# The pitch in DRAM between the rows of delta*u that one load of a selective scan reads

## The reference, cut to what matters

```python
delta = softplus(einsum('kblr,krc->kblc', dpart, dt_w) + 2 * dt_b)
# for each token, in the order of direction k:
dA    = exp(d[..., None] * A_neg)                 # A_neg = -exp(A_logs)
state = dA * state + (d * uu)[..., None] * b      # b: the token's 16 values of B
y     = einsum('kbcn,kbn->kbc', state, c)         # c: the token's 16 values of C
```

## Time and profile before

| | us |
|---|---|
| runs | 19140.31, 19143.47, 19148.17 |
| median | 19143.47 |
| profiled execution | 19173.11 |
| its span, from the first to the last instruction | 19171.4 |

### The profile page before, as it was taken

How to read it: one execution, slowest core, us unless ns; L and a number is a source line. 1 busy time by engine, 2 the same in 40 slices (tenths; PEclk the granted TensorE clock), 3 DMA queues, 4 the chain that set the end, 5 groups by cost and what they waited for, 6 DMA issues and landing times. The chain is left out here.

```text
span 19171.4 us, 359393 instructions
## 1 busy us (share of the span) xinstructions
PE 14991.3 (78%) x130080; PEld 11045.3 (58%) x130080; DVE 11710.9 (61%) x10632; ACT 7349.9 (38%) x12681; POOL 6928.4 (36%) x3199
## 2 busy tenths in 40 slices
PE   7899898989997534444888888888888888854489
PEld 5666666666665211122777677767777677732267
DVE  5666666666665666565667676667677667732232
ACT  4444444444443333333444444444444444411100
POOL 1000000000000233335777677767777677721100
PEclk9999999999998766676777777777777777765699
DMA  5222222222223555657999999899889999954411
GB/s 123 58 59 59 63 54 59 59 63 59 59 53 89 130 139 139 149 133 171 209 208 210 211 209 208 207 210 209 207 209 211 208 210 210 210 129 115 115 48 40
DMA packets 1692801, 2640.22 MB, mean 138 GB/s; under 512 B 1081676, under 2 KB 1245260, under 8 KB 1667404
## 3 DMA queue, kind: packets, MB, share of 16 engines
q1 hardware_dynamic: 1680332, 2551.26, 56.3%
q0 software_dynamic: 12288, 86.71, 2.1%
HBM read 2110.03 MB, written 556.32 MB: 139 GB/s over the span
## 5 line engine op out<-in xcount | busy, mean ns | idle before, releaser
L1680 DVE TENSOR_TENSOR_SCAN L2.h<-L2.ps,L2.db 128x912 f32<-128x912 f32 x2688 | 5514.0, 2056 | 2416.1 <-POOL L2.db L1545 2320.6
L1545 POOL TENSOR_TENSOR L2.db<-L2.du,L2.bt 128x896 f32<-128x896 f32 x2688 | 5576.7, 2093 | 2388.2 <-DMA L2.du<-du 2306.2
L1568 PE MATMUL L2.ps<-L2.dm,L2.wa 32*128 32x112 f32 (+2 forms) x24192 | 4522.0, 346 | 1132.1 <-DVE L2.h L1680 1005.5
L1568 PEld LDWEIGHTS L2.ps<-L2.dm,L2.wa 32*128 32x128 f32 x24192 | 4169.2, 258 | 1838.8 <-DVE L2.h L1680 1294.7
L1620 ACT ACTIVATE L2.ps<-L2.ps 128x896 f32<-128x896 f32 x2688 | 2426.0, 903 | 4607.2 <-PE L2.ps L1568 4606.8
L1580 PE MATMUL L2.ps<-L2.h,L2.cd 128*8 128x96 f32 x50176 | 2575.8, 362 | 4.2 <-DVE L2.h L1680 4.2
L1580 PEld LDWEIGHTS L2.ps<-L2.h,L2.cd 128*8 128x8 f32 x50176 | 1443.6, 108 | 583.8 <-DVE L2.h L1680 4.3
L1137 POOL TENSOR_TENSOR L2p.work<-L2p.work,L2p.xc 128x784 f32<-128x784 f32 x192 | 451.3, 2350 | 1659.2 <-DVE L2p.work L1300 1659.2
L314 POOL TENSOR_TENSOR L1.x_res<-L1.x_res,L1.ob 96x3136 f32 (+1 forms) x16 | 95.4, 5976 | 2584.8 <-ACT L1.qv L457 2584.8
L366 PE MATMUL L1.p_proj<-L1.xt,L1.w_hi 128*96 128x448 f32 x3024 | 826.9, 383 | 194.3 <-DVE L1.xt L560 167.4
L366 PE MATMUL L0.p_proj<-L0.xt,L0.w_hi 128*96 128x448 f32 x3024 | 824.2, 382 | 193.9 <-DVE L0.xt L560 167.4
(11 more groups left out here) (242 smaller groups left out, 20801.6 us busy)
## 6 DMA issues: line engine op xcount, KB each, us to landing
L2.du<-du SPq DMA_DIRECT2D x2688, 448.0 KB, 11.1
L2.dm<-d SPq DMA_DIRECT2D x896, 336.0 KB, 10.8
du<-L2p.work SPq DMA_DIRECT2D x128, 784.0 KB, 7.6
y<-L2.ysum SPq DMA_DIRECT2D x896, 84.0 KB
L0.left<-table SPq DMA_DIRECT2D x48, 1176.0 KB
L0.right<-table SPq DMA_DIRECT2D x48, 1176.0 KB
L1.left<-table SPq DMA_DIRECT2D x48, 1176.0 KB
L1.right<-table SPq DMA_DIRECT2D x48, 1176.0 KB
```

The source lines that it names most:

```text
L1545: pool.tensor_tensor(db[:, n % RB, :, 2:ROW], du[:, n % RD, :].rearrange("p (c t) -> p c t", t=SPAN), row, ALU.mult)\
L1568: mm = pe.matmul(decays[n % RA][:, a:b], wa[rows, j, :], dm[rows, j, a - lo:b - lo], start=True, stop=True)
L1680: dve.tensor_tensor_scan(h[:, half, u * UNIT:(u + 1) * UNIT, :].rearrange("p c t -> p (c t)"), decays[n % RA], db[:, n % RB, :, :].rearran ...
```

## The change

The tensor `du` is allocated with 896 floats (`UNIT * SPAN`, 3584 bytes) more behind each row of (direction, image, copy). The store and the load skip them. So the 16 rows of a load lie 2412032 bytes apart instead of 2408448. The same values are stored and read in the same order by the same instructions; the padding is never written or read. Tensors allocated after `du` move by 64 x 3584 bytes.

```diff
--- before.py
+++ after.py
@@ -1075,7 +1075,8 @@
                     sp.wait_ge(du_done, q)
                     for at, b, c, size in runs(pr, i):
                         for copy in range(COPIES):
-                            sp.dma_start(du_dram[k, b, copy, spans, c:c + size, :].rearrange("s c t -> c s t"),
+                            rows = du_dram[k, b, copy, 0:NSPANS * CH * SPAN].rearrange("(s c t) -> c s t", c=CH, t=SPAN)
+                            sp.dma_start(rows[c:c + size, spans, :],
                                          one[n % 2][at:at + size, span].rearrange("p (s t) -> p s t", t=SPAN))\
                                 .then_inc(du_stored[n % 2][half], 16)
                     sp.wait_ge(lo_done, q)
@@ -1451,7 +1452,7 @@
 
             def load_du(k, s, half, u):
                 c = half * HALF + u * UNIT
-                rows = du_dram[k].rearrange("b o s c t -> (b o) s (c t)")
+                rows = du_dram[k, :, :, 0:NSPANS * CH * SPAN].rearrange("b o (s n) -> (b o) s n", s=NSPANS)
                 rows = rows[:, s, c * SPAN:(c + UNIT) * SPAN] if isinstance(s, int) else \
                     rows[:, bass.ds(s, 1), c * SPAN:(c + UNIT) * SPAN].rearrange("r a n -> r (a n)")
                 src = bass.AP(tensor=rows.tensor, offset=rows.offset,
@@ -2050,7 +2051,7 @@
     z, xc = (nc.dram_tensor(n, (PAIRS, 128, 3, TOK), F32).ap() for n in ("z", "xc"))
     wa = nc.dram_tensor("wa", (DIRS, 128, SET * 128), F32).ap()
     d = nc.dram_tensor("d", (DIRS, NSPANS, SETS, 2, BATCH, SET, SPAN), F32).ap()
-    du = nc.dram_tensor("du", (DIRS, BATCH, COPIES, NSPANS, CH, SPAN), F32).ap()
+    du = nc.dram_tensor("du", (DIRS, BATCH, COPIES, NSPANS * CH * SPAN + UNIT * SPAN), F32).ap()
     bc = nc.dram_tensor("bc", (2, DIRS, BATCH, STATES, TOK), F32).ap()
     y = nc.dram_tensor("y", (DIRS, BATCH, TOK, CH), F32).ap()
     taps = [[nc.dram_tensor(f"taps{n}_{k}", (D1, LAGS), F32).ap() for k in range(2)] for n in range(2)]
```

## The result

| | before | after |
|---|---|---|
| median of the runs, us | 19142.56 (19132.33 to 19170.48, 8 runs) | 19199.33 (19181.35 to 19218.27, 8 runs) |
| profiled execution, us | 19173.11 | 19181.35 |

The ratio is 1.0029 [1.0018, 1.004]: the change makes the kernel 0.29% slower. The forecast was 17790.

What follows compares the result with a forecast made beforehand. DMA's handling of `du` was taken to bound the scan pass; with cheaper packets a half-span falls from 35.26 to 29.2 us (28.7 PE cycle, 0.5 SyncE), times 224 saves 1357 us: 17816, at the median's level 17790; range 17560 to 19200.

Steps and rivals of the forecast that it cites:

- What bounds the kernel: Scan pass: its end is set by how fast the DMA engines get through `du`, a full queue; half-span 35.26 us.
- (a): Stage before the pass: delta*u stores go to other addresses, hidden, taken as 0; 0.26 ms either way if not hidden.
- (b): `du` loads in the scan pass: the new pitch spreads the rows' addresses, a packet falls from 232 to 140 ns.
- 16 rows agree modulo 16384: `du` loads: at the old pitch all engines ask the same fraction of memory's parts, the supposed cause of 232 ns.
- burst of 140 ns: First `du` packets after the queue ran empty, 12104.6 to 12105.2: 140 ns each, taken as the unhindered price.
- Rival 2: `du` loads: nothing gained; limit on the writing side or in dealing 16 repeated rows to 128 partitions; chance 0.27.
- The Trainium skill's rule on pitches: Counter-evidence for `du` loads: only pitches of 2 MiB and up fell; by it the gain is 0, not 1.36 ms.
- Rival 3: `du` loads: spread rows serve engines unevenly, 6 ns more on the mean packet gives 19285 us; chance 0.13.
- The cycle through PE: Scan pass with cheap `du`: PE bounds next, six sum intervals 18.2 plus 10.5, so 28.7 us a half-span.
- four scans: Half-span after the sums: scans of units 9, 10, 11 and 0, 4 x 2.06 = 8.2 us of the 10.5.
- SyncE's order: Scan pass: y's stores and `cd` loads delay unit 4's `du` load; mostly hides, 0.5 us added, 29.2 in all.
- the 12.8 us to unit 4's landing: SyncE's queue after the last sum: 8.1 + 4.7 us remain; GpSimd at most about 2 us late, PE three units ahead.

Runs made afterwards that it cites:

- e1: Kernel before, each `du` load reading 128 different rows, one per partition, instead of 16 rows eight times each (other values reach the scan): 18591.58 us.
- q2: Kernel before with the eight `cd` loads moved in SyncE's list from behind unit 3's `du` load to behind unit 11's: 18605.79 us, ratio 0.9733.
- p2: Kernel before, stores and allocation kept, only the `du` loads reading at the new pitch (displaced values): 19206.01 us, ratio 1.003.
- e2: Kernel before, all 128 partitions of a `du` load reading one and the same 3584 bytes (other values reach the scan): 18757.47 us.
- e3: Kernel before, each `du` load reading 32 different rows, four times each, 688128 bytes apart (other values reach the scan): 18660.80 us.
- e4: Kernel before, each `du` load reading 16 rows eight times each, but rows lying 3584 bytes apart (other values reach the scan): 19043.16 us.
- s2: Kernel before with four copies of delta*u in DRAM, y's stores and `cd` loads spread behind units 5, 7, 9, 11: 18619.90 us, ratio 0.9728.
- r1: Kernel before with four copies of delta*u in DRAM instead of two, so loads read 32 rows four times each: 19361.35 us, ratio 1.0113.
- p1: Kernel before at the old pitch, with the padding all behind `du` so only later tensors move: 19144.59 us, ratio 0.9998.
- p0: The changed kernel run once more, against the kernel before: 19197.67 us, ratio 1.0022.
- r2: Kernel before with four copies of delta*u in DRAM and the change's 3584 bytes behind each row: 19522.39 us, ratio 1.0194.
- s1: Kernel before, y's stores and `cd` loads spread, one store and two loads behind units 5, 7, 9, 11: 18707.65 us, ratio 0.9769.

## Why the prediction was wrong, point by point

**What bounds the kernel: right in part.** `du`'s packets through the DMA engines hold the pass: cheaper ones gave 590 us of it in e1. But the queue wasn't full throughout: SyncE's order alone gave 565 us in q2, with `du` packets at the old price.

**(a), the stores at nothing: right.** GpSimd's first product starts at 8957.8 instead of 8962.1, and with the loads' pitch alone (p2) the whole slowdown is there.

**(b), 232 to 140 ns: wrong, and the step that sank the forecast.** At the new pitch a `du` packet costs what it did, 227 ns alone and 236.3 instead of 236.9 over the pass. I read "16 rows agree modulo 16384" as the cause since it held wherever 232 ns was seen. The number of outer rows and repeats held there too, and I had no row that parted the two. e2, e3 and e4 part them, all against me. The burst of 140 ns in the earlier trace rows was rightly what a `du` packet can take alone (141 ns in e2 and e3), but it says nothing on why it doesn't; and as the price of the whole pass it was too low, since e1's packets average 176 there. Rival 2 had the place: not the addresses, but how 16 repeated rows are dealt out to 128 partitions. Its evidence, `dm` at half rate, was in the prediction and deserved more than 0.27. It isn't as clean as I wrote, though: `dm`'s loads also read each of 32 rows twice (line 1442), so its 64 partitions alone aren't shown to be the cause. Whether it also gives the full rate with 32 rows depends on which engine fills which partitions, and that no run shows. The Trainium skill's rule on pitches, which spoke against me (DMA: Bandwidth & Descriptors, "Latency and other measured facts"), was right that this pitch has no large cost to mend, by e3 and e4; it holds nothing on the 0.3% of this pad or the 0.8% with four copies.

**Rival 3, slower: its sign was right, its place not.** It had `du` packets 6 ns dearer by uneven service, 19285 us. `du` stayed within 1 ns; `dm` rose by 9. I priced the pad only for the load that it belongs to, and not for the loads that run beside it. That 19199.33 lies within the stated range, 0.67 us under its upper end of 19200, is luck: the forecast was a gain, and nothing in its sum gives a loss of 57 us.

**The cycle through PE, 28.7 us: near, with its second half too short.** s2 came to 29.8 us a half-span in the mean and 29.25 in the median, with GpSimd's wait for `du` down to 179 us, though its `du` packets took 190 ns and not 140. Averaged over s2's trace, the six intervals with sums take 17.7 us, where I had 18.2, and the rest of the half-span 12.1, where I had 10.5. I let four scans set the pace of that rest. In the half-span shown it is mostly PE's own work, 10.53 of 12.03 us, with 27 decays at the low clock in 6.05 us and one wait for the scan of 1.5.

**SyncE's order, 0.5 us: mis-sized.** With cheap packets and the old order a half-span is 33.2 us (r1) and 32.6 (e1); spreading y and `cd` takes 3.4 us off r1 (s2). At the old packet price it is worth 2.5 (q2). I let the 12.8 us to unit 4's landing hide behind units in hand and looked at unit 4 alone; units 3, 4 and 5 all come late, by 2.4, 1.9 and 2.0 us on average in e1. The trace of before had it too, 1.0, 3.0 and 2.2 us at these units, had I averaged over all half-spans and not read one. Had (b) held, the change would have come near what e1 gave, 18592, and not 17790.

**Open:** what in 16 rows of 8 repeats costs the 90 ns, on the side that writes or in the dealing out; why 3584 bytes are worse than 0, 4096 or 32768, and whether `dm` alone pays for it; and which engine serves which partitions in the 16-row pattern.

## What to carry to other kernels

When a load reads a few rows many times over into 128 partitions, suspect the shape of its pattern before its addresses, and try it with another number of outer rows: 16 rows of 8 ran at 232 ns a packet, 32 of 4 at 141. A property that holds wherever the slowness is seen is no cause until a row or a run has it without the slowness. In a queue that is full on average, look for what is issued just before it runs dry: moving eight small loads out of the way gave 2.7%, nine times what the change's pitch cost.

## What the runs showed of the hardware, unexpected

- Loads whose 128 partitions all read the same 3584 bytes run at full rate while they are alone: 141 ns a packet, 419 GB/s (e2). Over the whole pass they are a little dearer than with 128 different rows: 190 ns against 176 (e1).
- 16 rows read 8 times each take 233 ns a packet alone (e4), 32 rows read 4 times each 141 (e3), with the same bytes, packet size and destination.
- With a pad of 3584 bytes in one tensor's pitch, packets read from another tensor were slower by 9 ns of 407 (before and p1 against after and p0); with 32 rows a load it made both kinds some 8 ns slower and cost 0.8% of the kernel (r1, r2).
- Large packets were dearer with small transfers spread among them: `du` packets took 237 ns with y's four stores and the eight `cd` loads each in one block (q2) and 253 with both spread (s1).
- Doubling 154 MB of stores in pieces of 448 bytes took 647 us of a stage whose DMA share had been 0.58 (r1).
